# Another order of the work in the tail of a two-layer graph network kernel

## The reference

```python
sim = jnp.tanh(adj * simlar)                 # here simlar is adj too
filt = sim * (adj > 0)
new_adj = top 350 of each row of filt        # here every row has fewer non-zeros
h2 = jnp.tanh(h @ W_proj + b_proj)
feat = jax.nn.relu(new_adj @ (h2 @ W_gcn) + b_gcn)
x = layernorm(x + feat)
```

## Time and profile before

| | us |
|---|---|
| median of three runs | 1399.0 |
| time of the profiled execution | 1400.07 |
| span of its profile | 1398.3 |
| start of the tail (first gate of round 0) | 1023.96 |
| first gate of round 4 | 1084.80 |
| first product of the graph | 1152.50 |
| last instruction of DVE | 1391.66 |

### The profile page before, as it was taken

The page is one execution under the profiler, slowest core; times in us unless marked ns, Lnnn a source line. Parts: engine busy times, 40 slices in busy tenths (PEclk is TensorE's granted clock), DMA queues, the critical chain, the costliest instruction groups (busy, mean ns, idle before and its releaser), DMA issues.

```text
span 1398.3 us, 11293 instructions
## 1 busy us (share of the span) xinstructions
PE 1349.2 (96%) x3716; PEld 627.6 (45%) x3716; DVE 1027.8 (74%) x1327; ACT 960.9 (69%) x1086; POOL 88.6 (6%) x188
## 2 busy tenths in 40 slices
PE   7999999989999999999999999999997889999996
PEld 3544444355444444444444444444443444444455
DVE  3244333436699998999989999899957885678883
ACT  4355445317688988889888898898935654556663
POOL 0000001000010010100100100101002430000000
PEclk9899999999999999999999999999999989999998
DMA  9687888244324242242323324223062006888860
GB/s 365 248 281 270 283 281 272 109 108 159 136 91 145 84 150 103 92 164 91 136 90 121 136 90 153 104 90 121 0 280 96 30 16 213 300 299 302 301 222 17
DMA packets 49321, 228.91 MB, mean 164 GB/s; under 512 B 10536, under 2 KB 20456, under 8 KB 23528
## 3 DMA queue, kind: packets, MB, share of 16 engines
q1 hardware_dynamic: 46688, 225.55, 46.1%
q10 hardware_dynamic: 2568, 2.58, 0.5%
HBM read 223.82 MB, written 4.29 MB: 163 GB/s over the span
## 4 chain that ended last, share of the span: by engine, by line
PE 67%; DVE 6%; POOL 3%; issue 1%; ACT 1%; DMA 1%; SPq 0%; POOLq 0%; DVEq 0%
PE t_y_ps L1689 46%; PE t_y_ps L1262 11%; PE t_y_ps L1667 4%; PE rows_ps L1262 2%; DVE mask L1140 2%; PE t_es_ps L1660 1%; DMA pieces<-scratch_ns_t 1%; PE t_y_ps L1213 1%; ACT pieces L1007 1%; POOL h_newton L960 1%; POOL h_newton L956 1%; POOL h_newton L958 1%; POOL h_root L962 1%; PE t_y_ps L1215 0%; DVE x_sb L1121 0%
## 5 line engine op out<-in xcount | busy, mean ns | idle before, releaser
L1689 PE MATMUL t_y_ps<-mask,x_sb 128*128 128x512 f32 x1536 | 663.0, 592 | 0.3 <-DVE mask L1607 0.3
L1689 PEld LDWEIGHTS t_y_ps<-mask,x_sb 128*128 128x128 f32 x1536 | 290.1, 190 | 364.0 <-issue 342.9
L1607 DVE TENSOR_TENSOR mask<-mask 128x1536 f32<-128x1536 f32 x256 | 449.0, 1755 | 2.0 <-ACT mask L1491 2.0
L1491 ACT ACTIVATE mask<-mask,ones 128x1536 f32<-128x1536 f32 x256 | 399.7, 1562 | 0.0
L1484 ACT ACTIVATE mask<-mask,pieces 128x512 f32<-128x512 f32 x352 | 241.3, 712 | 31.7 <-PE t_y_ps L1689 28.4
L383 PE MATMUL ns_ps<-pieces,x_sb 128*128 128x512 f32 x512 | 232.2, 609 | 10.0 <-DMA pieces<-in_adj_c 7.7
L1593 DVE TENSOR_SCALAR mask<-mask,e_cols 128x512 f32<-128x512 f32 x416 | 188.1, 484 | 56.7 <-PE t_y_ps L1689 45.7
L1262 PE MATMUL t_y_ps<-mask 128*128 128x512 f32 (+1 forms) x448 | 182.1, 565 | 0.0
L383 PEld LDWEIGHTS ns_ps<-pieces,x_sb 128*128 128x128 f32 x512 | 96.9, 194 | 133.1 <-issue 132.6
L210 ACT ACTIVATE signs<-pieces 128x2048 fp8e4<-128x2048 f32 x64 | 122.3, 1911 | 30.9 <-DMA pieces<-in_adj_c 15.7
L1140 DVE SCALAR_TENSOR_TENSOR mask<-mask 128x2048 f32<-128x2048 f32 x64 | 142.7, 2284 | 0.0
(11 more groups left out here) (163 smaller groups left out, 662.8 us busy)
## 6 DMA issues: line engine op xcount, KB each, us to landing
mask<-in_adj_c SPq DMA_DIRECT2D x128, 1024.0 KB, 4.8
pieces<-in_adj_c SPq DMA_DIRECT2D x64, 1024.0 KB, 4.9
mask<-scratch_shifts SPq DMA_DIRECT2D x8, 1536.0 KB, 7.7
mask<-in_x_t SPq DMA_DIRECT2D x1, 2048.0 KB, 16.4
scratch_ns_t<-ns_sb ACTq DMA_DIRECT2D x8, 256.0 KB, 5.9
pieces<-in_x_t SPq DMA_DIRECT2D x8, 256.0 KB, 2.9
pieces<-scratch_ns_t SPq DMA_DIRECT2D x8, 256.0 KB, 3.9
out<-x_sb SPq DMA_DIRECT2D x7, 256.0 KB, 6.4
```

Source lines behind the costliest of these rows:

```text
L1491: nc.scalar.activation(t, t, ACT.Exp, bias=ones[:, :], scale=-1.0).then_inc(exped, 1)
L1607: nc.vector.tensor_tensor(term(n), term(n), a, ALU.mult).then_inc(terms, 1)
L1689: mm = nc.tensor.matmul(y_ps[c % 2][h][:, :], x_sb[:, k, :], term(n)[:, h, :], start=k == 0, stop=k == NB - 1)
```

## The change

READY = 4 pieces are filtered in the rounds instead of seven, pieces 0 and 1 in round 0, 2 in round 1, 3 in round 2. SP issues four pieces, then each round's inputs with one piece behind them. `finish_x` of a chunk moves into the next round, `project` and `make_h2` a round later and to another place in it. Behind the rounds the order of what is left is new on all engines. In the last chunk DVE and ACT filter all eight pieces before `add_x1(6)`, `finish_y(6)`, `relu(6)` and `square_y(6)`, and PE's `turn_features(6)` comes behind the product of piece 60, not 58. No instruction is added or removed.

```diff
--- before.py
+++ after.py
@@ -859,6 +859,8 @@
 ROOT_SEED = 1597463007.0
 POOL_STEPS = 3 + 4 * NEWTON
 ROOT_ON_ACT = NCHUNK - 1
+READY = 4
+READY_IN = {0: (0, 1), 1: (2,), 2: (3,)}
 W_SLOT, IN_SLOT = 3, 4
 BUFFERS = ("edge_hid_n", "edge_r", "edge_z", "edge_n", "edge_cell", "both", "node_hid_n", "node_r",
            "node_z", "node_n", "node_cell", "squares")
@@ -967,11 +970,14 @@
             sp.dma_start(piece(u).rearrange("p (k n) -> p k n", n=CW), dram["adj_c"][c, :, g * PIECE:(g + 1) * PIECE, :]
                          ).then_inc(loaded[u % G_RING], 16)
 
-        for u in range(G_RING):
+        for u in range(READY):
             load_unit(u)
         for c in range(2, NCHUNK):
             sp.wait_ge(cells, c - 1)
             load_in(sp, c)
+            load_unit(READY + c - 2)
+        for u in range(READY + NCHUNK - 2, G_RING):
+            load_unit(u)
         for u in range(G_RING, NPIECES):
             sp.wait_ge(products, u - G_RING + 1)
             load_unit(u)
@@ -1047,40 +1053,48 @@
             if c == 0:
                 es_take_out(NCHUNK - 1)
             read_z("edge", c)
-            if c >= 2:
-                tanh(c - 2)
+            if c in (1, 2):
+                tanh(2 * (c - 1))
+            if c >= 3:
+                make_h2(c - 3)
             make_n("edge", c)
             read_hid("node", c)
             read_r("node", c)
+            if c == 1:
+                tanh(1)
+            if c >= 2:
+                copy_x(c - 2)
             if c >= 1:
                 square_x(c - 1)
-            if c >= 2:
-                copy_x(c - 2)
+            if c == 3:
+                tanh(3)
             read_z("node", c)
             make_n("node", c)
             if c >= 3:
                 copy_g(c - 3)
-            if c >= 2:
-                make_h2(c - 2)
-        copy_g(NCHUNK - 3)
-        copy_x(NCHUNK - 2)
-        tanh(NCHUNK - 2)
-        square_x(NCHUNK - 1)
-        make_h2(NCHUNK - 2)
-        tanh(NCHUNK - 1)
-        copy_x(NCHUNK - 1)
-        copy_g(NCHUNK - 2)
-        tanh(NCHUNK)
-        make_h2(NCHUNK - 1)
-        tanh(NCHUNK + 1)
-        copy_g(NCHUNK - 1)
-        for u in range(NCHUNK + 2, NPIECES):
+        end = NCHUNK - 1
+        make_h2(end - 2)
+        tanh(READY)
+        copy_x(end - 1)
+        copy_g(end - 2)
+        square_x(end)
+        make_h2(end - 1)
+        tanh(READY + 1)
+        copy_g(end - 1)
+        tanh(READY + 2)
+        copy_x(end)
+        tanh(READY + 3)
+        make_h2(end)
+        copy_g(end)
+        for u in range(NPIECE, NPIECES):
             tanh(u)
             c, g = divmod(u, NPIECE)
-            if c and g == 2:
+            if c < end and g == 2:
                 relu(c - 1)
-            if c and g == 4:
+            if c < end and g == 4:
                 square_y(c - 1)
+        relu(end - 1)
+        square_y(end - 1)
         for i in range(NCHUNK - 1, len(END_PARTS)):
             relu(i)
             square_y(i)
@@ -1174,27 +1188,35 @@
 
         for c in range(NCHUNK):
             pre_n("edge", c)
+            if c >= 2:
+                finish_x(c - 2)
             if c:
                 make_y(c - 1)
                 center(c - 1, x1[:, rows(c - 1), :], mean[:, rows(c - 1)], centered)
             make_cell("edge", c)
+            for u in READY_IN.get(c, ()):
+                square_a(u)
             pre_n("node", c)
             make_cell("node", c)
             add_cells(c)
-            if c:
-                finish_x(c - 1)
-                square_a(c - 1)
-        make_y(NCHUNK - 1)
-        center(NCHUNK - 1, x1[:, rows(NCHUNK - 1), :], mean[:, rows(NCHUNK - 1)], centered)
-        square_a(NCHUNK - 1)
-        finish_x(NCHUNK - 1)
-        for u in range(NCHUNK, NPIECES):
+        end = NCHUNK - 1
+        finish_x(end - 1)
+        square_a(READY)
+        make_y(end)
+        center(end, x1[:, rows(end), :], mean[:, rows(end)], centered)
+        square_a(READY + 1)
+        square_a(READY + 2)
+        finish_x(end)
+        square_a(READY + 3)
+        for u in range(NPIECE, NPIECES):
             square_a(u)
             c, g = divmod(u, NPIECE)
-            if c and g == 5:
+            if c < end and g == 5:
                 add_x1(c - 1)
-            if c and g == 7:
+            if c < end and g == 7:
                 finish_y(c - 1)
+        add_x1(end - 1)
+        finish_y(end - 1)
         for i in range(NCHUNK - 1, len(END_PARTS)):
             add_x1(i)
             finish_y(i)
@@ -1281,6 +1303,8 @@
                 combine(NCHUNK - 1)
             gate("edge", "z", c)
             gate("edge", "in_n", c)
+            if c >= 3:
+                project(c - 3)
             if c >= 1:
                 turn_cells(c - 1)
             pe.wait_ge(es_out, c + 1)
@@ -1292,29 +1316,31 @@
             gate("node", "in_n", c)
             if c >= 3:
                 features(c - 3)
-            if c >= 2:
-                project(c - 2)
-        features(NCHUNK - 3)
-        turn_cells(NCHUNK - 1)
-        turn_x(NCHUNK - 2)
+        end = NCHUNK - 1
+        project(end - 2)
         graph(0, 0)
-        project(NCHUNK - 2)
         graph(1, 0)
-        turn_x(NCHUNK - 1)
-        features(NCHUNK - 2)
+        turn_cells(end)
+        turn_x(end - 1)
+        features(end - 2)
         graph(2, 0)
-        project(NCHUNK - 1)
+        project(end - 1)
         graph(3, 0)
-        features(NCHUNK - 1)
+        features(end - 1)
+        turn_x(end)
+        graph(4, 0)
+        project(end)
+        graph(5, 0)
+        features(end)
         end = (NCHUNK - 1) * NPIECE
-        for u in range(4, end):
+        for u in range(6, end):
             c, g = divmod(u, NPIECE)
             graph(u, c)
             if c and g == 2:
                 turn_features(c - 1)
         for u in range(end, NPIECES):
             graph(u, NCHUNK - 1, 0, CHUNK // 2)
-            if u == end + 2:
+            if u == end + 4:
                 turn_features(NCHUNK - 2)
         for u in range(end, NPIECES):
             graph(u, NCHUNK, CHUNK // 2, CHUNK)
```

## The result

The changed kernel takes 1382.18 us in the median of four runs (1380.64 to 1383.44), the kernel before 1398.71 beside it: a ratio of 0.9877, 95% interval 0.9865 to 0.9888. Its profiled execution took 1383.14 us, with a span of 1381.5.

A forecast was written before the change was run, and what follows sets the result against it. In the rounds neither TensorE nor VectorE is full, and VectorE's order makes the wait. 5.4 + 15.0 - 0.5 - 1.6 - 1.8 = 16.5 us saved, 1382.4 us on the median of 1399.0; range 1376.5 to 1390.

The forecast's parts named there:

- Part 1: Rounds 0 to 3, inputs between pieces: the 7.47 us gap before round 2 goes, but VectorE is late; gain 5.4 us.
- Part 2: Rounds 4 to 7 without squares: TensorE sets the pace at 12.95 us a round; gain 15.0 us.
- Part 3: Between graph(0) and piece 6: the last root, held by VectorE's squares, stalls TensorE 1.95 us; loss 0.5 us.
- Part 4: Last chunk: TensorE stands 4.2 us before turn_features(6), waiting for the moved relu(6); loss 1.6 us.
- Part 5: TensorE's lower clock behind the new gaps, counted behind those of 1.9 and 1.95 us; loss 1.8 us.
- VectorE did not set rounds 4 to 7: Rival: VectorE still sets the rounds, period 14.0 instead of 12.95 us, 4.2 worse, 1386.6 us; chance 0.2.
- the clock did not stay down: Rival: after the gaps of rounds 1 to 3 TensorE stays at 1.2 GHz through rounds 4 to 7, 1435 us; chance 0.03.
- the inputs were in time: Rival: round 2's inputs stay late because SP's issue waits for add_cells(0); rounds shift by 4, 1386 us; chance 0.05.
- No charge at all: Rival: clock stays up through short gaps and in the end, GpSimd not held; 1376.8 us, half 1379.5; chance 0.2.
- the sign: Whole kernel: faster means under 1396.2 us; chances faster 0.94, same 0.03, slower 0.03.
- the second rival: Second in the list: no charge for clock or held GpSimd, 1376.8 us; chance 0.2.
- the first: First rival in the list: VectorE still sets rounds 4 to 7, 4 x 1.05 = 4.2 us worse; chance 0.2.

The follow-up runs named there:

- a6_root_first: Changed kernel with finish_x(7) ahead of the squares of pieces 5 and 6 on VectorE, copy_g(6) and copy_x(7) ahead of their tanh on ACT; 1381.28 us.
- a4_finish_back: Changed kernel with finish_x back at the end of its own round on VectorE, squares staying in rounds 0 to 2; 1386.61 us.
- b1_finish_only: Kernel before with only finish_x of a chunk moved into the next round on VectorE; 1392.26 us.
- a1_old_end: Changed kernel with the last chunk back in the old order on ACT, DVE and PE; 1379.76 us.
- a2_relu_early: Changed kernel with relu(6) alone moved back to behind the tanh of piece 58 on ACT; 1376.84 us.
- a3_pieces_first: Changed kernel with SyncE's old order, 11 pieces first and the inputs behind them; 1384.87 us.

## Why the prediction was right, step by step

The number, 1382.4 against 1382.18, is better than its parts, which erred both ways: by the table the tail gained 17.2 us against a sum of 16.5, and it began 0.4 us later. The mechanisms of parts 1 to 4 held; that the total fits to 0.2 us is luck.

- **Part 1 (5.4 us, measured 4.25).** The mechanism held: the earlier trace rows gave `add_cells(0)` at 20.38 us from the first gate, and it started at 20.38 (1044.75); the gap ahead of it was 2.61 against 2.9. `add_cells(1)` came at 33.69 (33.7 forecast). Round 2 began 28.47 us from the first gate, 1.7 later than forecast, by the low clock behind the first gap; the second gap was 0.65 us for that reason, not 2.6, and the third 2.10 against 1.9. The step that failed is the period of 14.00 for round 2: it was 15.18 (1058.06 to 1073.24). VectorE's rows show what is in it:

```profile
1058.06 0.69 DVE L1129 TENSOR_TENSOR pieces<-pieces 128x512 f32<-128x512 f32 x1
...
1060.89 0.69 DVE L1149 TENSOR_TENSOR x_sb<-x_sb,h_root 128x512 f32<-128x512 f32 x1 [0.82 <-POOL h_root L965]
...
1073.24 0.69 DVE L1129 TENSOR_TENSOR pieces<-pieces 128x512 f32<-128x512 f32 x1 [0.46 <-DVE pieces L1122]
```

`finish_x(0)` waited 0.82 us for the root, though I had called it free because the 15 steps would have had a round's time. GpSimd's rows for that root, and the same `finish_x(0)` in a6_root_first, where the clock behind the first gap was full:

```profile
1054.63 0.19 POOL L953 TENSOR_SCALAR h_newton<-h_square_sums 128x4 f32<-128x4 f32 x1 [80.72 <-ACT pieces L1013]
...
1058.10 0.70 POOL L961 TENSOR_TENSOR h_newton<-h_newton,h_var 128x4 f32<-128x4 f32 x1
...
1060.65 0.20 POOL L965 TENSOR_TENSOR h_root<-h_root,h_newton 128x4 f32<-128x4 f32 x1
```

```profile
1061.48 0.69 DVE L1149 TENSOR_TENSOR x_sb<-x_sb,h_root 128x512 f32<-128x512 f32 x1 [0.23 <-POOL h_root L965]
```

The root began at 1054.63 and was asked for 5.4 us later, not a round's time, and it took 6.22 us instead of 4.18, because VectorE's instructions held some of its steps (0.5 to 0.7 us each instead of 0.2), which I had reckoned with at the last root only. The low clock added to it: it made the node gates late, with them ACT's tanh of piece 1 and, behind that, `square_x(0)`, 1.7 us later from the first gate than in a6_root_first. So "absorbed by the next gap" was true of TensorE's own time and not of those behind it. In a6_root_first the wait was 0.23 us and the period 14.60 (1059.23 to 1073.83): of the 1.2 us too much about half is the clock's, and the other half is there without it. A further 0.46 us before `add_cells(2)` has no releaser but VectorE itself; it stands in a6_root_first and a4_finish_back too, so it isn't the clock's, and stays open.
- **Part 2 (15.0, measured 15.12).** 4 rounds of 12.93 and `project(5)`. a4_finish_back and b1_finish_only show that both periods in the sum, 14.0 with a square and under 12.95 without, were right.
- **Part 3 (loss 0.5, measured 0.53).** The gap was 1.82 against 1.95. That the running square holds GpSimd is now shown by a6_root_first: 6.34 us against 4.18, and the gap gone. The rule of the Trainium skill (GPSIMD Engine Reference, section 1: interfaces shared with VectorE, contention with instructions that have two inputs from SBUF) agrees with these rows; without it the forecast had been 2 us too low here.
- **Part 4 (loss 1.6, measured 1.45).** The gap was 4.02 against 4.2, and the low clock behind it came (7.03 against 7.13).
- **Part 5 (loss 1.8, measured 0 where it was charged).** This term failed. No stretch at the lower clock stood where I charged one, in round 3 or behind `turn_x(7)`; one stood behind `turn_cells(0)`, where I had called it free and it cost some 0.6 us (the distance from the first gate to the third gap's end is 49.62 us, and 49.03 in a6_root_first, which had none there); that cost is part of part 1's 4.25. This term and the miss of part 1, 1.15 us, offset each other.
- **Rivals.** VectorE did not set rounds 4 to 7, the clock did not stay down, and the inputs were in time. "No charge at all" was half right, for the clock in round 3 and behind the last root only. On the sign, the forecast speaks of a lag four times the second rival's; that rival has none, and what is meant is a lag of 13.8 us, over three times the 4.2 of the first.

## What to carry to other kernels

Ask of each moved instruction which engine sets the pace where it lands: two squares cost 1.4 us in rounds with 1.1 us of slack each, and four cost 8.75 us in the three rounds that VectorE sets. Where an in-order engine works ahead, everything that another engine waits for must go before that work: one `relu` behind five more tanh turned a gain of about 3 us into a loss. Two periods, each engine's own sum and each loop through several engines, foretold rounds 4 to 7 to 0.1 us a round. They missed round 2 by 1.2 us: by a root whose steps VectorE held, and by the clock.

## What was not expected of the hardware

- A gap of about the same length is followed by the lower clock in one profile and not in another: before piece 61, 2.5 us of idle and then 7.13 us for 24 records, but 5.59 in a1_old_end; behind a gap of 2.61 us a granted clock of 0.62, and full in a6_root_first. What a stretch cost differed too. From `turn_features(6)` to the second half of the last chunk are 5.62 us in a2_relu_early, without a gap; behind the gap of 4.0 us they were 6.99 in a6_root_first, 7.36 in the changed kernel, and 8.23 in a3_pieces_first:

```profile
1349.40 1.12 PE L1291 MATMUL t_y_ps<-ident,pieces 128*128 128x128 f32 x4 [4.02 <-ACT pieces L1037]
...
1350.31 7.48 PE L1281 MATMUL rows_ps<-mask 128*128 128x256 f32 x24
```

- A GpSimd step of 0.2 us on 128x4 elements can last until the VectorE instruction beside it ends: 2.12 us beside a `square_a` of 2.28, and 0.5 to 0.7 beside the 512-column steps of 0.69 of `make_cell`, `add_cells` and `pre_n`.
